# Layer 0's attention: the copy of a group's outputs one unit of squares later, and their turn one unit later

## The chip, the cores and the metric

One core of a Trainium2 chip runs the whole program. The metric is the time of one execution on the device in microseconds (us). The engines are named as in the profile: PE is TensorE (PEld its weight loads), ACT is ScalarE, DVE is VectorE, POOL is GpSimd, SP the queue that issues DMAs.

## What is computed

The program is two layers of a small model. Only the attention of layer 0 is touched: 1024 tokens, 16 heads of 16 columns, fourth-degree polynomial scores with a causal mask.

```python
a = jnp.einsum('bhnd,bhmd->bhnm', q, k) ** 4
a = jnp.tril(a)
denom = jnp.sum(a, axis=-1, keepdims=True)
out = jnp.einsum('bhnm,bhmd->bhnd', a / denom, v)
out = out.transpose(0, 2, 1, 3).reshape(b, n, e) @ w_out
```

After it come the mix into x, a layer norm, layer 1's attention and its mixture of experts. They wait for the attention's output.

## The kernel before

**Units.** The heads are worked in four groups g of four heads. A group has eight rows R = 8g + j, one for each block of 128 keys; row j needs queries from block j on. A row is cut into units: two heads by half of the row's width for j below 4, two heads by the whole width for j 4 and 5, four heads for j 6 and 7. There are 22 units in a group and 88 in all. A unit n passes through these steps:

- TensorE computes its scores into one of three pairs of PSUM banks (`scores0`, L609).
- ScalarE squares them out of PSUM into SBUF (L1109; semaphore `s0_sq`).
- VectorE squares the squares in place (L1437). For three units of a group ScalarE does it instead (L1112), always after it has done the next unit's first square.
- GpSimd masks the diagonal block of a unit that has one (L1818).
- TensorE multiplies a finished row by V (`out0`, L629) in two halves of the queries. It accumulates the group's outputs in banks 6 and 7.

**The end of a group.** ScalarE copies the group's outputs from banks 6 and 7 to `o_raw` (`copy_out0`, L1083). The first output product of the next group overwrites those banks, so `out0` waits for the copy (`o0_copied`). TensorE then turns `o_raw` in `turn_out0`: it takes a bank pair, runs `keep_clock(2, b)` (two matmuls nobody reads, four rows at L573), waits for the copy and does eight transposes (L641). VectorE divides by the denominators (`read_out0`, L1418 and L1420; `o0_ready`). When two groups are done, `turn_o(0)` turns their finished columns (L652), ScalarE's `high_o` and VectorE's `low_o` split the result in two parts (L1089, L1427; `oT_ready`). `add_nothing` (L578) adds products of zero to keep TensorE busy.

**The order.** `order0` writes TensorE's order out by hand: after the scores of unit n comes at most one output product. The output products of a row come LAG = 4 units after its last unit. `turned[n + 3]` places the turn. `PAIRED0` lists all steps that take a bank pair (scores, turn, turn_o) in TensorE's order, and the pairs rotate by three, so each step waits until the third before it has been read: scores by the square, a turn by `o0_ready`, a turn_o by `oT_ready`. ScalarE and VectorE run through the units in number order, with the special steps put in by dictionaries that are worked out from the same list: `COPY_AT` (ScalarE copies just before the square of that unit), `READ_AT` (VectorE divides just after that unit) and `SPLIT_O_AT` (both engines split just after that unit).

In the text s48 stands for the scores of unit 48 and q48 for their square on ScalarE; 4th47 is the fourth power of unit 47 on ScalarE, out16.0 the first half of row 16's output product, T1 the turn of group 1. Units 44 to 65 belong to group 2; unit 48, before whose square the copy of group 1 stands, is the first of group 2's second row, because the products run four units late.

Of the kernel before, what the change touches and what calls it, by code (L numbers as in the profile page):

```python
# [18 lines left out]
NT = TOK // P  # L19
# [7 lines left out]
H0, D0 = 16, 16  # L27
STK = 4 * D0
QUAD = 4
# [6 lines left out]
def units0(j):  # L36

    w = (NT - j) * P
    size = 2 if j < 6 else 4
    cuts = [(0, w // 2), (w // 2, w)] if j < 4 else [(0, w)]  # L40
    return [(list(range(i, i + size)), a, e) for i in range(0, QUAD, size) for a, e in cuts]


UNITS0 = [(R, *unit) for R in range(ROWS0) for unit in units0(R % NT)]
# [7 lines left out]
def order0():  # L52

    out, pieces, used, turned = [], [], None, {}
    for n in range(len(UNITS0) + LAG + 4):
        if n < len(UNITS0):
            out.append(("scores", n))
        for R in range(ROWS0):
            if DONE0[R] + LAG == n + 1:
                pieces += [("out", R, half) for half in range(NHALF) if R % NT < 4 * half + 4]  # L60
        for piece in pieces[:1 if n < len(UNITS0) else len(pieces)]:
            out.append(pieces.pop(0))
            if piece[1] % NT == NT - 1:
                turned[n + 3] = piece[1] // NT
        if n in turned:
            out.append(("turn", turned[n]))
            if turned[n] == H0 // QUAD // NC - 1:
                used = n + 4
        if n == used:
            out.append(("turn_o", 0))  # L70
    return out + [("turn", H0 // QUAD - 1)] * (("turn", H0 // QUAD - 1) not in out) + [("turn_o", 1)]


ORDER0 = order0()
PAIRED0 = [s for s in ORDER0 if s[0] != "out"]
PAIR_OF = {s: n % 3 for n, s in enumerate(PAIRED0)}


def last_scores(step):

    return max((s[1] for s in ORDER0[:ORDER0.index(step)] if s[0] == "scores"), default=0)


COPY_AT = {min(last_scores(("out", NT * g + NT - 1, 1)) + 1, len(UNITS0)): g for g in range(H0 // QUAD)}
READ_AT = {last_scores(("turn", g)): g for g in range(H0 // QUAD - 1)}
SPLIT_O_AT = last_scores(("turn_o", 0)) + 1
OUT_BANKS = [6, 7] + [2 * (3 - PAIR_OF["turn", H0 // QUAD - 1] - PAIR_OF["turn_o", 1]) + i for i in range(2)]
# [67 lines left out]
def build_program(nc, x_in, wqkv_in, wout_in, lns_in, lnb_in, packed_in, scales_in,  # L155
# [5 lines left out]
    with ExitStack() as ctx:  # L161
# [811 lines left out]
        def _(act):  # L973
# [105 lines left out]
            def copy_out0(g):  # L1079
                act.wait_ge(o0_used, NT * (g + 1))  # L1080
                if g >= 1:
                    act.wait_ge(o0_turned, g)
                act.activation(o_raw[:], psf[:, 3072:4096], ACT.Copy)\  # L1083
                    .then_inc(o0_copied, 1)
# [9 lines left out]
            for n in range(len(UNITS0)):  # L1094
                R, heads, a, e = UNITS0[n]
                w = e - a
                if n in COPY_AT:
                    copy_out0(COPY_AT[n])
                act.wait_ge(s0_ps, n + 1)
# [982 lines left out]
```

## Time and profile before

| what | value |
|---|---|
| time, median of 3 runs | 838.12 us (834.84, 838.12, 838.96) |
| time of the profiled execution | 838.65 us |
| its span, first to last instruction | 836.9 us |
| layer 0's attention stage in the span, about | 196.8 to 300.6 us |
| copies of the outputs (L1083) start at | 223.4, 248.4, 273.0, 295.2 us |

The time of an execution stands 1.75 us above its span; that part lies around the program. The three runs shown differ by 4.1 us, or 0.5%.

### The profile page before, as it was taken

What the parts mean: (1) busy time and instruction counts of PE and PEld (TensorE: products, weight loads), DVE (VectorE), ACT (ScalarE), POOL (GpSimd) and SP (SyncE); (2) the same over time, 40 slices, a digit from 0 to 9 for tenths busy, and PEclk for the clock granted to TensorE, in tenths of its full rate; (3) what the DMA queues carried; (4) which work ended last, traced back from release to release, by engine and by line L of the source; (5) the groups of instructions that cost most, each with busy time, mean ns of one, the idle gap of its engine ahead of it and who ended that gap; (6) DMA issues with size and microseconds to landing.
All of it is one profiled execution on the core that took longest, in us unless ns stands there. A gap on an engine that the chain in (4) does not pass through costs nothing.

```text
span 836.9 us, 14053 instructions
## 1 busy us (share of the span) xinstructions
PE 790.9 (95%) x4927; PEld 645.2 (77%) x4927; DVE 607.8 (73%) x1077; ACT 466.2 (56%) x822; POOL 424.0 (51%) x479
## 2 busy tenths in 40 slices
PE   6999999998889889998999999999999999999997
PEld 5777777765433367797999889989999999988885
DVE  8588869648989968778888688887767654445556
ACT  4433242359888833687656456655666655655431
POOL 1757846613554446455345433758565512655540
PEclk9999999999999999999999999999999999999999
DMA  5211186000000040000000000102010587743207
GB/s 186 69 45 38 39 255 182 1 1 1 1 1 2 1 129 26 26 7 26 7 20 7 8 20 7 58 26 65 21 51 26 200 200 266 279 149 104 57 2 251
DMA packets 50116, 59.82 MB, mean 71 GB/s; under 512 B 13559, under 2 KB 41084, under 8 KB 50048
## 3 DMA queue, kind: packets, MB, share of 16 engines
q1 hardware_dynamic: 45488, 50.49, 19.7%
q0 software_dynamic: 4560, 8.44, 2.8%
q8 instruction: 41, 0.67, 0.3%
q14 instruction: 27, 0.22, 0.1%
HBM read 41.11 MB, written 21.86 MB: 75 GB/s over the span
## 4 chain that ended last, share of the span: by engine, by line
PE 54%; DVE 11%; POOL 6%; ACT 6%; issue 4%; DMA 3%; SPq 0%; POOLq 0%; ACTq 0%; DVEq 0%
PE ps L802 12%; PE ps L517 8%; PE ps L519 8%; PE ps L518 8%; PE ps L895 4%; PE ps L926 3%; PE ps L892 3%; POOL A L1818 2%; DVE cap L1511 2%; DVE swap L1500 2%; PE ps L713 2%; PE ps L874 1%; DMA xa<-xg_scratch 1%; PE ps L559 1%; ACT A L1109 1%
## 5 line engine op out<-in xcount | busy, mean ns | idle before, releaser
L802 PE MATMUL ps<-V,P 128*128 128x129 f32 x1152 | 151.0, 277 | 0.0
L1161 ACT ACTIVATE cap<-cap 128x1024 f32<-128x1024 f32 (+7 forms) x128 | 87.3, 682 | 112.4 <-DVE cap L1511 106.9
L802 PEld LDWEIGHTS ps<-V,P 128*128 128x128 f32 x1152 | 143.6, 192 | 2.7
L1511 DVE SCALAR_TENSOR_TENSOR cap<-dist,ps 128x1024 f32<-128x1024 f32 (+7 forms) x128 | 95.4, 750 | 26.3 <-PE ps L519 22.9
L1742 POOL TENSOR_SCALAR_AFFINE_SELECT P<-P 128x128 f32<-128x128 f32 x128 | 39.4, 308 | 143.2 <-ACT P L1166 142.7
L1874 POOL DMA_INDIRECT y_scratch<-y_sb,aux_s x63 | 62.1, 985 | 61.8 <-issue 33.1
L1166 ACT ACTIVATE P<-cap 128x1024 f32<-128x1024 f32 (+7 forms) x128 | 87.9, 687 | 4.1
L517 PE MATMUL ps<-q_hi,k_hi 128*128 128x512 f32 x192 | 72.1, 376 | 6.8 <-DVE cap L1511 6.2
L519 PE MATMUL ps<-q_lo,k_hi 128*128 128x512 f32 x192 | 67.3, 351 | 0.0
L518 PE MATMUL ps<-q_hi,k_lo 128*128 128x512 f32 x192 | 66.9, 349 | 0.0
L517 PE MATMUL ps<-xT_hi,w_hi 128*128 128x512 f32 x128 | 56.4, 441 | 2.9 <-POOL w_lo L1762 1.9
L1667 DVE TENSOR_SCALAR gu<-ps 128x256 f32<-128x256 f32 (+1 forms) x63 | 28.9, 459 | 38.4 <-PE ps L895 15.9
L1849 POOL TENSOR_TENSOR rot<-rot,swap 128x512 f32<-128x512 f32 x40 | 52.1, 1302 | 8.7 <-DVE swap L1500 8.6
L1050 ACT ACTIVATE e_g<-ps 128x512 f32<-128x512 f32 x32 | 19.2, 599 | 66.2 <-PE ps L519 66.2
L1500 DVE TENSOR_TENSOR swap<-ps,sin 64x512 f32<-64x512 f32 x80 | 55.1, 688 | 1.1
L1437 DVE TENSOR_TENSOR A<-A 128x1024 f32<-128x1024 f32 (+2 forms) x40 | 49.6, 1287 | 4.5 <-ACT A L1109 4.5
L519 PE MATMUL ps<-xT_lo,w_hi 128*128 128x512 f32 x128 | 50.6, 395 | 0.0
L518 PE MATMUL ps<-xT_hi,w_lo 128*128 128x512 f32 x128 | 50.5, 394 | 0.0
L1198 ACT ACTIVATE sg<-gu 128x128 f32<-128x128 f32 (+1 forms) x63 | 20.5, 325 | 50.9 <-DVE gu L1667 46.3
L1109 ACT ACTIVATE A<-ps 128x1024 f32<-128x1024 f32 (+2 forms) x48 | 43.6, 967 | 9.1 <-PE ps L609 9.1
L517 PEld LDWEIGHTS ps<-q_hi,k_hi 128*128 128x128 f32 x192 | 36.5, 190 | 12.9 <-DVE cap L1511 4.8
L1857 POOL TENSOR_TENSOR q_lo<-rot,q_hi 128x512 fp32r<-128x512 f32 x32 | 41.4, 1293 | 9.0 <-ACT q_hi L1155 8.9
(293 smaller groups left out, 2100.6 us busy)
## 6 DMA issues: line engine op xcount, KB each, us to landing
xg_scratch<-blank SPq DMA_DIRECT2D x1, 8127.0 KB, 31.2
xa<-xg_scratch SPq DMA_DIRECT2D x63, 128.0 KB
ew<-in_experts SPq DMA_DIRECT2D x3, 1920.0 KB, 8.9
y<-y_scratch SPq DMA_DIRECT2D x8, 512.0 KB
pk<-in_packed SPq DMA_DIRECT2D x8, 384.0 KB, 3.1
pks<-in_scales SPq DMA_DIRECT2D x8, 384.0 KB, 4.0
ew<-in_experts SPq DMA_DIRECT2D x1, 3072.0 KB
wqk<-in_wqk SPq DMA_DIRECT2D x20, 128.0 KB
```

The source lines that it names most:

```text
L517: pe.matmul(o, l_hi, r_hi, start=start, stop=False)
L518: pe.matmul(o, l_lo, r_hi, start=False, stop=False)
L519: return pe.matmul(o, l_hi, r_lo, start=False, stop=stop)
L802: last = pe.matmul(ps[:, 4 + r % 2, o:o + D1 + 1], P1[:, h % 2, a:a + P], V1[:, j, h // REP, :], start=(j == 0), stop=(j == t))
L1109: act.activation(dst, src, ACT.Square).then_inc(s0_sq, 1)
L1161: act.activation(cap[:, CAP_AT[j]:CAP_AT[j] + w], cap[:, CAP_AT[j]:CAP_AT[j] + w], ACT.Tanh, scale=1.0 / (CAP * float(D1) ** 0.5))\
L1166: act.activation(P1[:, h % 2, OFF[j]:OFF[j] + w], cap[:, CAP_AT[j]:CAP_AT[j] + w], ACT.Exp, scale=CAP)\
L1437: dve.tensor_tensor(a, a, a, ALU.mult).then_inc(s0_four, 1)
L1500: last = dve.tensor_tensor(swap[to, i % 2, :], b[frm, :], sin1[frm, tk], ALU.mult)
L1511: dve.scalar_tensor_tensor(out=cap[:, CAP_AT[j]:CAP_AT[j] + w], in0=dist[:, 0:w], scalar=slope, in1=psf[:, 1024 * (n % 2):1024 * (n % 2) + ...
L1849: pool.tensor_tensor(r, r, swap[:, i % 2, :], ALU.add).then_inc(pj_rot, 1)
L1874: pool.indirect_dma_start(out=y_dram, out_offset=bass.IndirectOffsetOnAxis(ap=aux_s[:, b, 0:1].bitcast(U32), axis=0), in_=y_sb[:, b % YRIN ...
```

## The change

The turn of groups 0 to 2 goes one unit later in TensorE's order. The first output product of the next group has a fixed place, so it now stands ahead of the turn. ScalarE's copy goes one unit later: one more square is done ahead of it. The last group's copy and turn stand where they stood, because its place is cut off at the number of units. What follows from the order moves too:

| | before | after |
|---|---|---|
| copy ahead of the square of unit | 26, 48, 70, 88 | 27, 49, 71, 88 |
| TensorE around T1 | s48 s49 s50 T1 s51 out16.0 s52 out16.1 s53 | s48 s49 s50 s51 out16.0 T1 s52 out16.1 s53 |
| VectorE divides after unit | 28, 50, 72 | 29, 51, 73 |
| turn_o(0) in TensorE's order | s54 turn_o s55 out17.0 s56 | s54 s55 out17.0 turn_o s56 |
| both engines split after unit | 55 | 56 |

Units 29, 51 and 73 are fourth-powered by ScalarE, so VectorE has no work of its own between the two places, and its division stands where it stood.

```diff
             if piece[1] % NT == NT - 1:
-                turned[n + 3] = piece[1] // NT
+                turned[n + 4] = piece[1] // NT
...
-COPY_AT = {min(last_scores(("out", NT * g + NT - 1, 1)) + 1, len(UNITS0)): g for g in range(H0 // QUAD)}
+COPY_AT = {min(last_scores(("out", NT * g + NT - 1, 1)) + 2, len(UNITS0)): g for g in range(H0 // QUAD)}
```

## Rows read from the trace of the kernel before

**Rows 1.** The page: busy us (share of the span) and instructions of each engine.
```profile
PE 790.9 (95%) x4927; PEld 645.2 (77%) x4927; DVE 607.8 (73%) x1077; ACT 466.2 (56%) x822; POOL 424.0 (51%) x479
```

**Rows 2.** Busy time of each engine from copy 1 to copy 2.
```profile
core 0: us, PE busy (x) PEld busy (x) DVE busy (x) ACT busy (x) POOL busy (x), PEclk, DMA share, GB/s
248.40:273.00 24.60, 21.84 (x172) 9.37 (x170) 22.51 (x24) 21.84 (x30) 12.15 (x15) 1.00 0.00 1
```

**Rows 3.** The chain that ended last, over the stage: start, us, what.
```profile
261.06 2.30 DVE stack L1437 x3
...
264.76 4.83 POOL A L1818 x4
...
272.98 0.26 ACT o_raw L1083
```

**Rows 4.** Timeline of ACT around copy 1: start, us, instruction [idle before <-releaser].
```profile
248.37 1.02 ACT L1083 ACTIVATE o_raw<-ps 128x1024 f32<-128x1024 f32 x1
249.28 0.92 ACT L1109 ACTIVATE A<-ps 128x896 f32<-128x896 f32 x1
250.07 1.07 ACT L1112 ACTIVATE A<-A 128x1024 f32<-128x1024 f32 x1
251.02 2.59 ACT L1109 ACTIVATE A<-ps 128x896 f32<-128x896 f32 x3
254.06 0.81 ACT L1109 ACTIVATE qk_tok<-ps 128x768 f32<-128x768 f32 x1 [0.45 <-PE ps L609]
...
255.61 2.38 ACT L1109 ACTIVATE qk_tok<-ps 128x768 f32<-128x768 f32 x3
```

**Rows 5.** Timeline of PE around T1.
```profile
248.09 0.92 PE L609 MATMUL ps<-QT,KT 64*128 64x448 f32 x6
250.25 1.13 PE L573 MATMUL ps<-x_tok 128*128 128x256 f32 x4 [1.25 <-ACT A L1109]
251.22 1.04 PE L641 MATMUL ps<-ident,o_raw 128*128 128x128 f32 x8
252.18 0.47 PE L609 MATMUL ps<-QT,KT 64*128 64x448 f32 x2
252.58 1.06 PE L629 MATMUL ps<-A,V 128*32 128x512 f32 x8
253.58 0.44 PE L609 MATMUL ps<-QT,KT 64*128 64x384 f32 x2
```

**Rows 6.** Timeline of PE, ACT and DVE around turn_o(0) and its split.
```profile
257.07 0.85 PE L629 MATMUL ps<-A,V 128*32 128x384 f32 x8
257.89 1.08 ACT L1089 ACTIVATE xT_hi<-ps 128x512 fp32r<-128x512 f32 x2
258.51 1.29 DVE L1427 TENSOR_TENSOR xT_lo<-ps,xT_hi 128x512 fp32r<-128x512 f32 x2 [0.23 <-ACT xT_hi L1089]
258.84 0.73 ACT L1109 ACTIVATE stack<-ps 128x640 f32<-128x640 f32 x1
...
259.43 0.87 ACT L1112 ACTIVATE qk_tok<-qk_tok 128x768 f32<-128x768 f32 x1
...
259.86 0.71 PE L609 MATMUL ps<-QT,KT 64*128 64x320 f32 x6 [0.60 <-DVE xT_lo L1427]
260.32 1.90 ACT L1109 ACTIVATE stack<-ps 128x640 f32<-128x640 f32 x3
```

**Rows 7.** Timeline around T0, the same steps a group earlier.
```profile
225.29 1.75 PE L573 MATMUL ps<-x_tok 128*128 128x256 f32 x4 [1.25 <-ACT A L1109]
226.84 1.92 PE L641 MATMUL ps<-ident,o_raw 128*128 128x128 f32 x8
...
230.73 0.81 ACT L1109 ACTIVATE qk_tok<-ps 128x768 f32<-128x768 f32 x1 [0.44 <-PE ps L609]
```

**Rows 8.** A window around T0; the columns of rows 2.
```profile
226.00:229.00 3.00, 3.00 (x13) 2.35 (x11) 2.44 (x3) 1.80 (x3) 0.41 (x1) 0.50 0.00 0
```

**Rows 9.** Timeline of ACT behind T2.
```profile
278.68 0.81 ACT L1109 ACTIVATE qk_tok<-ps 128x768 f32<-128x768 f32 x1 [0.45 <-PE ps L609]
```

## The prediction

> **What bounds the kernel now.** I read the page first: PE is busy for 95% of an 836.9 us span [rows 1], but that is a mean over stages. So I asked for the stage that the change touches, from one copy of a group's outputs to the next. In those 24.6 us PE is busy for 21.84 us, DVE for 22.51 us and ACT for 21.84 us [rows 2]. No engine is the bound alone, so the chain of work that ended last has to say what the order costs. It leads from the copy through ACT and PE to VectorE's fourth powers at 261.06, from there on through DVE and four masks on POOL (4.83 us), and so to the next copy at 272.98 [rows 3]. Two things follow. What delays the fourth powers at 261.06, or their like in another group, delays the group by as much, since DVE runs on without idle time behind them. And what ACT loses ahead of them is not made up, since the squares feed DVE one by one. Behind the stage all work waits for its last output, so a microsecond lost here is one lost in the end.
>
> Then the timelines of ACT and PE around copy 1 [rows 4, 5]. ACT has no idle time from 248.37 to the end of its three squares at 251.02 + 2.59 = 253.61; it stands for 0.45 us before q52. PE stands for 1.25 us before T1, because T1's bank pair is the one that q48 reads, and q48 comes behind the copy. I call the distance from one start to the next on an engine the step of an instruction: it is shorter than the record, since these overlap.
>
> **The change around copy 1, step by step.** Nothing is added or removed; it is the same instructions in another order.
>
> - *ACT.* q48 needs s48, which PE starts at 248.09; two such matmuls take 0.47 us and an activation starts 0.04 us behind them (253.58 + 0.44 to 254.06) [rows 4, 5]. So q48 starts at 248.60 where the copy started at 248.37. 4th47 follows after q48's step of 0.79, at 249.39, the copy after another 0.95, at 250.34. It ends at 251.36; it ended at 249.39. The three squares q49 to q51 start 0.91 later, at 251.25, and end at 253.84, which is 0.23 later than before.
> - *PE.* s51 takes a pair that q48 frees at 249.52, so it is done inside the wait, by 250.04. This step of 0.40 (252.18 to 252.58) is what the new order gains. But the next instruction in the queue is out16.0, and it needs banks 6 and 7, which are free only when the copy ends: 251.36 and 0.05 for the release (250.20 to 250.25 before) gives 251.41 [rows 4, 5]. All that is queued behind waits with it. Then out16.0 takes its step of 1.00, keep_clock 0.97 and the transposes 0.96 [rows 5]. T1's own wait is for q49, over at about 252.2, so it costs nothing. s52 starts at 251.41 + 2.93 = 254.34, where it started at 253.58: later by 0.76. The short form: PE's work starts 1.16 us later and has 0.40 us less to do.
> - *Who waits.* q52 goes to 254.82; ACT's idle time before it grows from 0.45 to 1.0 us. VectorE's division follows T1 with nothing moved past it, and what waits for it is s54, two units of scores further on. No DMA is issued by any moved step, and no queue of SP or POOL is passed.
>
> So a group whose turn is moved loses **0.76 us** up to its fourth powers. In group 2 the picture of before is the same, down to the 0.45 us of idle time [rows 9], so T2 costs 0.75 us as well.
>
> **Around T0** the clock comes in. PE's granted clock is 0.50 from 226 to 229, and 1.00 over all of the next group [rows 2, 8]: TensorE ran at 1.2 GHz there and at 2.4 GHz here. keep_clock's and the transposes' records are 1.75 and 1.92 us long there, against 1.13 and 1.04 around T1 [rows 5, 7]. From the copy to the unit behind the turn it is 230.73 - 223.41 = 7.32 us, and 254.06 - 248.37 = 5.69 us around T1 [rows 4, 7]: such a fall costs 1.63 us. What PE did before it fell is the same as around T1: a wait of 1.25 us and then keep_clock. If the clock falls at the same instant in the changed kernel, out8.0 starts at 223.41 + 3.04 = 226.45 and has a step of 2.0 at 1.2 GHz, keep_clock starts at 228.45. The low clock lasts to about 229.1 (the transposes' end is at 228.76, and the window at 229 still shows it), so 0.64 us of keep_clock run at it, which is 0.32 of its work of 0.97, and 0.65 are left at the full one, then 0.96 for the transposes and 0.44 for s30: 231.14. q30 starts at 231.18, against 230.73: **0.45 us** lost where a fall is there before and after, and 0.75 where there is none in either.
>
> **The turn of the finished columns** moves too, and this is the dearest part. After T1's delay, q52 stands at 254.82 and q53 1.55 behind it, at 256.37 (254.06 to 255.61); 4th51, which runs between them, ends as q53 starts, by 256.5 [rows 4]. turn_o now comes behind out17.0. That product needs 4th51, and its record is 0.85 long, so turn_o starts at 257.3; it is eight transposes as T1 is (a step of 0.96), so s56 starts at 258.3 and q56 about 0.45 behind it, at 258.8, where it was [rows 6]: up to here the delay is made up, because the split no longer stands ahead of q56. But 4th55 now comes ahead of the split as well. It starts 0.59 behind q56 (258.84 to 259.43), at 259.4, and ScalarE's split 0.77 later (0.87 of record less 0.1), at 260.14, where it started at 257.89. VectorE's part ends 1.91 behind that (257.89 to 259.80), at 262.05. Its end frees the bank pair: before for s57 at 259.86, after for s58. So s58 starts at 262.11, and q58 at 262.56 (0.46 behind, as 260.32 behind 259.86), where q58 stood 0.6 behind 260.32, at 260.91. ACT stands idle for 0.8 us in front of it. The fourth power of unit 58 stood second of the three that take 2.30 us, at about 261.06 + 0.74 = 261.80. It now follows q58's end, 262.56 + 0.70, at 263.3: 1.5 us later, and DVE goes on from there [rows 3, 6]. The 0.76 of T1 are contained in this, so group 1 loses **1.5 us**.
>
> **Sum.** 0.45 + 1.5 + 0.75 = 2.7 us. The last group and its end are unchanged. Against the profiled execution this is 838.65 + 2.7 = 841.35 us. That execution stands 0.53 us above the median, so on the median it is 838.12 + 2.7 = **840.8 us**, or 0.3% slower. What measurement can tell from no change here is about 0.5%, or 4.2 us. The two unknown sizes are bounded so: a plain turn costs between 0 (PE's work fits into the wait) and 1.16 (nothing of it is gained), the split between 0.76 (only T1's delay goes on) and 2.25 (its whole shift from 257.89 to 260.14 goes on). That is 0.8 to 4.6 us for the three; I take the values read off step by step, as every step of them has a row of its own shape beside it.
>
> **Rivals.**
>
> - *The clock falls more often* (slower; the other side of no difference). Between s50's end at 249.0 and out16.0 at 251.41 PE now has 1.9 us without work, with only s51 inside, where it had 1.25 us. The row shows that 1.25 us was enough around T0 and not around T1 and T2, so the place is close to the edge already. Each further fall costs 1.63 us less the 0.3 that T0's delay shrank by, so 1.3 to 1.6: 842.3 with one, 843.7 with two. It decides from the first further fall on, since 2.7 + 1.5 reaches 4.2 us. For it speaks the longer idle time in all three places; against it that keep_clock still stands right behind. The Trainium skill ("TensorE: Matmul & The Clock Gate", A second HAM failure mode: psum-queue depth-cycling) says that short idles of PE between groups of matmuls, as it cycles through PSUM banks, are enough to make the clock oscillate. By that rule, the trace agrees at one place in three. Chance 0.25.
> - *The clock no longer falls.* The matmuls of s51 now stand inside the wait and may keep it up around T0. Then 838.12 + 0.75 + 1.5 + 0.75 - 1.63 = 839.5 us. Against it speaks that the idle time in all is longer. Chance 0.10.
> - *Something else sets the group's length.* If POOL's four masks (4.83 us) with DVE beside them had slack ahead of them, the delay would end there and nothing would change: 838.1 us. The chain speaks against it: it passes from DVE to POOL without an idle piece [rows 3]. Chance 0.10.
> - *Faster.* The old copy stood ahead of q48 and made PE wait 1.25 us. If TensorE's early scores were worth more than I count, at best all 0.45 us of ACT's idle time at three places and the one fall would go, 3.0 us: 835.1 us. It would need out16.0 not to wait for the copy. Chance 0.05.
> - *The forecast*, with as many falls as before: 0.50.
>
> **Range and chances.** From 838.0, the case that nothing changes, to 843.5, nearly two further falls, it holds all but the faster case and the far ends. Slower by over 0.5% is above 842.3: most of the first rival and the upper end of the forecast's bounds, 0.25. Faster by over 0.5% is below 833.9, which no case reaches, 0.04 for what I have not seen. Within 0.5% is 0.71.
>
> **What would show it.** In the profile after, the first instruction of PE behind the copy must be L629, waiting for the copy, 3.0 us after the end of q47; the square behind the turn must stand 6.45 us after the old place of the copy (5.69 before). In group 1 the six score matmuls at 259.86 no longer wait for xT_lo; the next ones do, and ACT idles 0.8 us there. The distance between the copies must grow by 0.75 and 1.5. A granted clock of 0.50 around T1 or T2 would speak for the first rival. The prediction is wrong if the distance between copies stays at 24.6 us though PE waits longer.

## The result and the profile after

The changed kernel takes 843.1 us in the median of 11 runs (839.83 to 846.94), the kernel before 837.41 us in 11 (833.97 to 841.85). The ratio is 1.0072, with a 95% interval of 1.0052 to 1.0093: slower by 6.0 us, between 4.4 and 7.8. The forecast was 2.7 us slower. The time lies in the stated range, near its upper end (843.5). It is beyond what the prediction counted as no difference (842.3), a case to which it had given a chance of 0.25, against 0.71 for no difference.

The profiled execution after took 846.91 us, one of the slowest of the 11. The page:

```profile
span 845.2 us, 14053 instructions
PE 793.5 (94%) x4927; PEld 646.3 (76%) x4927; DVE 604.9 (72%) x1077; ACT 465.8 (55%) x822; POOL 425.5 (50%) x479
```

As many instructions as before and nearly the same busy time in each engine; the span is longer by waits [rows 1]. Around T1, PE's timeline after; these are the lines that answer to [rows 5]:

```profile
247.29 0.90 PE L609 MATMUL ps<-QT,KT 64*128 64x448 f32 x6
248.78 0.47 PE L609 MATMUL ps<-QT,KT 64*128 64x448 f32 x2 [0.59 <-ACT A L1109]
250.64 1.07 PE L629 MATMUL ps<-A,V 128*32 128x512 f32 x8 [1.38 <-ACT o_raw L1083]
251.63 1.13 PE L573 MATMUL ps<-x_tok 128*128 128x256 f32 x4
252.60 1.04 PE L641 MATMUL ps<-ident,o_raw 128*128 128x128 f32 x8
253.57 0.45 PE L609 MATMUL ps<-QT,KT 64*128 64x384 f32 x2
```

s51 runs inside the wait, out16.0 waits 1.38 us for the copy, and then everything follows with the steps of before. ACT's timeline at the same place answers to [rows 4]:

```profile
248.62 1.05 ACT L1112 ACTIVATE A<-A 128x1024 f32<-128x1024 f32 x1
249.57 1.01 ACT L1083 ACTIVATE o_raw<-ps 128x1024 f32<-128x1024 f32 x1
250.47 2.53 ACT L1109 ACTIVATE A<-ps 128x896 f32<-128x896 f32 x3
254.05 0.81 ACT L1109 ACTIVATE qk_tok<-ps 128x768 f32<-128x768 f32 x1 [1.05 <-PE ps L609]
```

From 4th47 to q52 it is 254.05 - 248.62 = 5.43 us; the prediction had 254.82 - 249.39 = 5.43. ACT's idle time before q52 is 1.05 us, as forecast (1.0; it was 0.45).

At the split of the turned columns, PE, ACT and DVE after; the answer to [rows 6]:

```profile
259.40 1.08 ACT L1089 ACTIVATE xT_hi<-ps 128x512 fp32r<-128x512 f32 x2
260.02 1.29 DVE L1427 TENSOR_TENSOR xT_lo<-ps,xT_hi 128x512 fp32r<-128x512 f32 x2 [0.40 <-ACT xT_hi L1089]
...
261.37 0.30 PEld L609 LDWEIGHTS ps<-QT,KT 64*128 64x128 f32 x4 [2.23 <-DVE xT_lo L1427]
261.37 0.56 PE L609 MATMUL ps<-QT,KT 64*128 64x320 f32 x4 [2.00 <-DVE xT_lo L1427]
261.83 1.30 ACT L1109 ACTIVATE stack<-ps 128x640 f32<-128x640 f32 x2 [0.75 <-PE ps L609]
...
263.15 1.93 PE L629 MATMUL ps<-qk_tok,V 128*32 128x512 f32 x8
```

The wait for xT_lo stands in front of s58 as forecast and costs ACT 0.75 us of idle time (forecast 0.8). But look at PE: it stands for 2.00 us there, and two instructions on, the product at 263.15 has a record of 1.93 us, where its like takes 1.06 [rows 5]. That is the clock, which the windows show (columns of [rows 2]):

```profile
225.50:228.00 2.50, 2.50 (x11) 0.96 (x4) 2.09 (x2) 1.87 (x3) 0.05 (x1) 0.50 0.00 0
250.50:254.50 4.00, 3.86 (x30) 2.11 (x30) 2.88 (x4) 2.95 (x5) 0.75 (x2) 1.00 0.01 2
262.60:265.60 3.00, 3.00 (x12) 0.81 (x14) 2.75 (x3) 1.55 (x2) 0.93 (x1) 0.50 0.00 0
279.60:282.60 3.00, 3.00 (x12) 2.30 (x10) 1.43 (x2) 0.92 (x2) 0.41 (x1) 0.50 0.00 0
```

PE ran at 1.2 GHz at T0, at the split of group 1 and at T2, and at 2.4 GHz at T1. Before it ran at 1.2 GHz at T0 alone [rows 2, 8]. I call a stretch with a granted clock of 0.50 a low window, and what begins it a fall of the clock.

I measure the stage from the start of the first score matmul to the start of the last copy. Before, that is 98.4 us (from 196.8 to 295.2, the last time in the table above). After:

```profile
L609 PEld LDWEIGHTS ps<-QT,KT x192: 182/183/334, 195.3 to 293.5; 64*128 64x128 f32 x192
L1083 ACT ACTIVATE o_raw<-ps x4: 1015/1016/1024, 223.9 to 299.7; 128x1024 f32<-128x1024 f32 x4
```

With two decimals of the timelines it is 299.68 - 195.34 = 104.3 us, against 98.38 before: 6.0 more. All stages below are taken with two decimals. The two traces differ by 8.3 us in their spans. The rest lies outside the stage: it begins 1.5 us earlier after, and behind it 3.8 us more were spent. The changed lines do not reach those parts. In the nine traces of this document the part behind the stage takes 537.7 to 545.5 us, and it is not long where the stage is long (539.0 behind the longest stage, of 110.4). So I don't explain that rest by the change.

### The profile page after: what moved, and what is told of

Its sections match the earlier page's. It is cut to its first block, busy times and chain, and to the rows that moved or that the text cites. A ratio compares the mean times of both kernels' runs of the same rounds, so it can differ in the third digit from the quotient of the medians.

```text
span 845.2 us, 14053 instructions
## 1 busy us (share of the span) xinstructions
PE 793.5 (94%) x4927; PEld 646.3 (76%) x4927; DVE 604.9 (72%) x1077; ACT 465.8 (55%) x822; POOL 425.5 (50%) x479
## 4 chain that ended last, share of the span: by engine, by line
PE 56%; DVE 11%; ACT 6%; POOL 6%; issue 5%; DMA 1%; SPq 0%; POOLq 0%; ACTq 0%; DVEq 0%
PE ps L802 12%; PE ps L517 8%; PE ps L519 8%; PE ps L518 8%; PE ps L895 4%; PE ps L892 3%; PE ps L926 2%; DVE cap L1511 2%; DVE swap L1500 2%; PE ps L629 2%; POOL A L1818 2%; PE ps L713 2%; PE ps L559 1%; PE ps L874 1%; POOL rot L1849 1%
## 5 line engine op out<-in xcount | busy, mean ns | idle before, releaser
L1511 DVE SCALAR_TENSOR_TENSOR cap<-dist,ps 128x1024 f32<-128x1024 f32 (+7 forms) x128 | 95.3, 750 | 25.6 <-PE ps L519 22.1
```

What stands on the lines that cost most here:

```text
L1511: dve.scalar_tensor_tensor(out=cap[:, CAP_AT[j]:CAP_AT[j] + w], in0=dist[:, 0:w], scalar=slope, in1=psf[:, 1024 * (n % 2):1024 * (n % 2) + ...
```

## The experiments

The theory that stood at the outset: the order costs 3.0 us where no fall of the clock is counted (0.75 + 1.5 + 0.75), and the rest of the 6 us is TensorE's clock, which falls more often because PE has longer idle time. The rival is that the longer waits, or the copy's or the turn's place, cost more by themselves than the steps say. A stage without a fall takes 98.4 - 1.63 = 96.75 us in the kernel before by this theory. The experiments were timed in two sets, each beside 29 runs of the kernel before: the first four with a median of 835.88 us for that kernel, the last three with 836.94 us. Each ratio is to the kernel before of its own set.

### The copy alone later

```diff
-                turned[n + 4] = piece[1] // NT
+                turned[n + 3] = piece[1] // NT
```

(Against the changed kernel.)

> The copy one unit later alone; TensorE's order stays as in the kernel before. Reading by order: T1 gets its pair from q48 at 249.5 and runs keep_clock while the copy runs, so its transposes start when the copy ends (251.4) and all behind it is 0.2 us later per group, 0.6 us in the stage. From the stage's first scores to the last copy 97.3 us without a fall of the clock (96.75 before, worked out as 98.38 less one fall of 1.63), plus 1.6 per fall. Ratio 1.000 to 1.002. The rival that the copy's place itself is what costs: ratio near 1.004 or more.

Measured: ratio 0.9991, interval 0.9975 to 1.0008. The stage in its trace, and PE at T1:

```profile
L609 PEld LDWEIGHTS ps<-QT,KT x192: 182/183/187, 195.7 to 287.0; 64*128 64x128 f32 x192
L1083 ACT ACTIVATE o_raw<-ps x4: 1016/1017/1024, 224.3 to 293.2; 128x1024 f32<-128x1024 f32 x4
```
```profile
248.95 1.09 PE L641 MATMUL ps<-ident,o_raw 128*128 128x128 f32 x8 [0.73 <-ACT o_raw L1083]
249.97 0.47 PE L609 MATMUL ps<-QT,KT 64*128 64x448 f32 x2
```

The stage takes 97.5 us, with a granted clock of 1.00 in all its windows. The forecast was 97.3. PE waits in two parts with keep_clock between them. So the copy's place costs 0.7 us of order and no clock in this trace, and nothing that the timing can tell. The rival that blames the copy falls.

### The turn alone later

```diff
-COPY_AT = {min(last_scores(("out", NT * g + NT - 1, 1)) + 2, len(UNITS0)): g for g in range(H0 // QUAD)}
+COPY_AT = {min(last_scores(("out", NT * g + NT - 1, 1)) + 1, len(UNITS0)): g for g in range(H0 // QUAD)}
```

> The turn one unit later alone, with turn_o(0) and its split moved as in the changed kernel; ScalarE's copy stays in its old place. Reading by order: out16.0 finds the copy done, s51 and out16.0 run before T1 instead of behind it, and s52 starts where it did: T0 and T2 cost nothing. The split still comes behind q56 and 4th55 and costs 0.7 us in group 1. Stage 97.5 us without falls, 1.6 more per fall; PE keeps its 1.25 us wait at each turn and gets a wait of about 2 us at the split, where a fall is likely. Ratio 1.001 to 1.003. Rival (the turn's place costs by itself): 0.75 per group, stage 99 us and over.

Measured: 1.0076, interval 1.0048 to 1.0103 (6 runs). That is the whole loss again, against my expectation of 1.001 to 1.003. PE at T1:

```profile
250.38 0.91 PE L609 MATMUL ps<-QT,KT 64*128 64x448 f32 x6
252.54 0.47 PE L609 MATMUL ps<-QT,KT 64*128 64x448 f32 x2 [1.25 <-ACT A L1109]
253.68 1.93 PE L629 MATMUL ps<-A,V 128*32 128x512 f32 x8 [0.68 <-ACT A L1112]
255.54 2.08 PE L573 MATMUL ps<-x_tok 128*128 128x256 f32 x4
257.41 1.91 PE L641 MATMUL ps<-ident,o_raw 128*128 128x128 f32 x8
259.26 0.69 PE L609 MATMUL ps<-QT,KT 64*128 64x384 f32 x2
```

The copy starts at 250.66 in this trace and is over at 251.68, so out16.0 does not wait for it. It waits for its other input, 4th47 (L1112), and starts 253.68 - 250.66 = 3.02 us behind the copy's start: just when it would in the changed kernel (251.41 - 248.37 = 3.04 in the prediction's times). ScalarE does the copy, q48 and 4th47 in either kernel before out16.0 can start, and only their order differs. I had overlooked that wait. Then out16.0, keep_clock, the transposes and s52 all run at 1.2 GHz. Four windows, one at each of the three turns and one at the split:

```profile
224.00:230.00 6.00, 4.26 (x19) 1.71 (x16) 4.77 (x5) 5.03 (x6) 1.61 (x4) 0.65 0.00 0
251.00:257.00 6.00, 4.07 (x18) 1.60 (x16) 4.58 (x4) 4.85 (x6) 1.44 (x4) 0.68 0.00 1
265.00:271.00 6.00, 4.00 (x24) 1.26 (x24) 4.14 (x6) 4.32 (x7) 1.34 (x2) 0.65 0.00 0
282.00:288.00 6.00, 4.30 (x17) 1.56 (x16) 4.62 (x5) 5.26 (x7) 1.33 (x4) 0.66 0.01 3
```

The mean clock is about 0.66 in all four. The stage takes 110.4 us (197.24 to 307.65). This trace is of the slowest of the six runs, 848.34 us; their median is 843.34.

### turn_o(0) and its split back at their old places

```diff
-                used = n + 4
+                used = n + 3
```

> The changed kernel with turn_o(0) and the split at their old places (behind s54 and unit 55). Reading by order: group 1 loses 0.76 instead of 1.5 us, so the stage is 99.0 us without falls; against the changed kernel's trace the distance from copy 1 to copy 2 falls from 27.5 to about 25.4 us, since the 2 us wait of PE at the split and the fall in it go too. Ratio 1.003 to 1.006 with two falls left. If the split costs nothing by itself, the distance stays within 0.3 us of 27.5.

Measured: 1.0033, interval 1.0013 to 1.0054. From copy 1 to copy 2 it is 26.6 us; after it was 27.5. A fall stands inside the distance (the window at T1):

```profile
251.50:254.50 3.00, 2.49 (x10) 0.74 (x11) 1.79 (x3) 2.88 (x4) 0.72 (x2) 0.51 0.00 0
```

The fall of the changed kernel stood at the split and this one stands at T1, so this pair of traces has a fall on both sides, and 0.9 us is what the split costs beside it. That bears out the sign; the size needs a kernel without falls (below). My 25.4 us had none in it; with a fall of 1.6 us it would be 27.0, so the trace is 0.4 us shorter. The whole stage is 104.8 us in this trace, no shorter than in the changed kernel, because the clock was low for longer at T0: from T0's copy to T1's it is 27.0 us, against 25.6 in the changed kernel. So no gain shows in this one trace; the timed runs show one, though the two intervals touch (1.0013 to 1.0054 here, 1.0052 to 1.0093 for the changed kernel).

### The waits filled

The changed kernel, with two matmuls nobody reads ahead of s29, s51, s73 and s57. They write to the bank pair that those scores overwrite.

```diff
-                bank_pair(("scores", n))
+                keep_clock(2 * (n in (29, 51, 57, 73)), bank_pair(("scores", n)))
```

> The changed kernel with two matmuls nobody reads ahead of s29, s51, s73 (inside the wait for the copy) and ahead of s57 (inside the wait for the split): about 1 us of idle time of TensorE is filled at each of the four places, nothing else waits for them. If the excess over the 3.0 us of the order is clock (three falls in the trace after, one before): no window of granted clock 0.50 in the stage, stage 99.8 us instead of 104.3, ratio 1.001 to 1.003. If the longer waits cost the excess without the clock: the stage stays near 104 us, ratio 1.007.

Measured: 1.0028, interval 1.001 to 1.0046. Windows over the stage, and its ends:

```profile
196.00:224.00 28.00, 24.41 (x173) 9.49 (x172) 24.91 (x24) 24.73 (x33) 13.89 (x15) 1.00 0.00 1
224.00:250.00 26.00, 23.37 (x172) 10.12 (x172) 23.37 (x23) 22.60 (x29) 13.79 (x15) 1.00 0.00 1
250.00:277.00 27.00, 24.07 (x184) 10.83 (x186) 22.74 (x24) 22.82 (x30) 13.68 (x16) 1.00 0.01 2
277.00:299.00 22.00, 20.62 (x162) 9.44 (x155) 16.15 (x18) 14.66 (x20) 9.03 (x11) 1.00 0.08 16
```
```profile
L609 PEld LDWEIGHTS ps<-QT,KT x192: 182/183/187, 196.7 to 290.5; 64*128 64x128 f32 x192
L1083 ACT ACTIVATE o_raw<-ps x4: 1016/1017/1024, 225.3 to 296.6; 128x1024 f32<-128x1024 f32 x4
```

The clock is 1.00 throughout and the stage takes 99.9 us; 99.8 was expected. The matmuls that nobody reads take 4.4 us out of the stage. What PE waits for comes no earlier for it:

```profile
250.47 1.07 PE L629 MATMUL ps<-A,V 128*32 128x512 f32 x8 [0.33 <-ACT o_raw L1083]
261.19 0.56 PE L609 MATMUL ps<-QT,KT 64*128 64x320 f32 x4 [0.94 <-DVE xT_lo L1427]
```

The copy starts at 249.40 here, so out16.0 starts 1.07 us behind it, as in the changed kernel (250.64 - 249.57), and s58 starts 11.8 us behind it, as there (261.37 - 249.57). The order's delays are still there and only their idle time is partly filled, so it was the clock and not the waits that made the difference. Over the runs, the mean granted clock of this kernel is 0.9962, that of the kernel before beside it 0.9960: with the clock no lower it is still 2.3 us slower (0.8 to 3.8). That is the order's part, 3.2 us in the traces.

### The turn alone, filled

As the turn alone, with such pairs of matmuls, fillers from here on, ahead of s28, s50, s72 and s57.

> The turn alone one unit later (as in the run with the copy in its old place), with two matmuls nobody reads ahead of s28, s50, s72 and s57, so that the clock stays up. Its unfilled form showed out16.0 starting 3.03 us behind the copy's start, held by the fourth power of unit 47 on ScalarE, not by the copy: as late as in the changed kernel (3.04). If that is the cost of the order, the stage takes about 99.9 us here (96.75 + 0.75 + 1.5 + 0.75 and a little for the fillers), as with the changed kernel filled, ratio 1.002 to 1.004, and all the rest of the 110.4 us of the unfilled form was clock. If the turn's place costs nothing by itself (my first reading), the stage takes 97.5 us, ratio 1.000 to 1.001.

Measured: 1.0026, interval 1.0006 to 1.0045; stage 100.1 us, against 110.4 unfilled. So 10.3 us of that stage were clock, and the turn's place costs as much order as turn and copy together. Over the runs the gain is smaller: the kernel is 0.76% slower than the one before without the fillers and 0.26% with them, which is some 4 us. PE at T1:

```profile
249.10 1.07 PE L629 MATMUL ps<-A,V 128*32 128x512 f32 x8 [0.71 <-DVE A L1437]
```

The copy starts at 246.04 here; out16.0 starts 3.06 us behind it. The profile puts the wait down to VectorE's fourth power of unit 48, which ends then. The code does not wait for that unit. 4th47 ends 0.3 us earlier, at 248.81, and is the only input of out16.0 that ends late; the unfilled trace names it. I take it to be the cause by the code, and did not test it by itself.

### turn_o(0) back, filled

> The changed kernel with turn_o(0) and its split at their old places and fillers ahead of s29, s51, s73. If the place of the split costs 0.75 us by itself, the stage takes 99.1 to 99.2 us without falls (99.93 with the split moved) and the distance from copy 1 to copy 2 is 25.4 to 25.5 us (26.26 with it moved). If the split costs nothing once the clock is kept, the stage stays at 99.9. Ratio 1.001 to 1.003.

Measured: ratio 1.0016, interval 0.9996 to 1.0037. The stage:

```profile
L609 PEld LDWEIGHTS ps<-QT,KT x192: 182/183/187, 196.7 to 289.5; 64*128 64x128 f32 x192
L1083 ACT ACTIVATE o_raw<-ps x4: 1015/1016/1024, 225.4 to 295.7; 128x1024 f32<-128x1024 f32 x4
```

That is 98.9 us. From copy 1 to copy 2 it is 25.2 us, against 26.3 us with the split moved and filled. The split's place costs 1.0 us by itself, forecast as 0.75. This kernel has no filler ahead of s57, but that one delays nothing in the other (s58 starts at the same distance from the copy with it and without it, above).

### The kernel before, filled

```diff
-                bank_pair(("scores", n))
+                keep_clock(2 * (n in (28, 50, 72)), bank_pair(("scores", n)))
```

> The kernel before with two matmuls nobody reads ahead of s28, s50 and s72, inside the wait of 1.25 us. If one fall costs 1.63 us and nothing else changes, the stage takes 96.8 us instead of 98.38, and the median is up to 1 us below the one before, which has such a fall in some of its runs only: ratio 0.9985 to 1.000. If the fillers delay the turn, the stage is longer than 96.9 us without a fall and the ratio is 1.000 or above.

Measured: 0.999, interval 0.997 to 1.0009. The stage:

```profile
L609 PEld LDWEIGHTS ps<-QT,KT x192: 182/183/187, 195.4 to 286.0; 64*128 64x128 f32 x192
L1083 ACT ACTIVATE o_raw<-ps x4: 1019/1022/1024, 222.0 to 292.1; 128x1024 f32<-128x1024 f32 x4
```

That is 96.7 us, as the 96.75 worked out for the kernel before without its fall. It bears out the price of the fall at T0: 98.38 - 96.74 = 1.64 us. Over the runs, the mean granted clock of the whole program is 0.9978 with the fillers and 0.9958 without them, a share worth 1.7 us. The median is 0.95 us lower, and the interval holds no difference at all, so no kernel here beats the one before measurably.

All stages side by side, in us, each from one trace; the last column is the mean granted clock of the whole program, over all runs of the kernel that have it on record:

| kernel | stage | granted clock of 0.50 in it | mean clock of the runs |
|---|---|---|---|
| before | 98.4 | T0 | 0.9960 and 0.9958 (29 each) |
| before, filled | 96.7 | nowhere | 0.9978 (12) |
| copy alone | 97.5 | nowhere | 0.9969 (12) |
| turn_o back, filled | 98.9 | nowhere | 0.9977 (12) |
| changed, filled | 99.9 | nowhere | 0.9962 (12) |
| turn alone, filled | 100.1 | nowhere | 0.9976 (12) |
| changed | 104.3 | T0, split, T2 | 0.9924 (11) |
| turn_o back | 104.8 | T0 (long), T1, T2 | 0.9944 (12) |
| turn alone | 110.4 | all four, long | 0.9887 (6) |

## Why the prediction was right, and where it fell short

**The order's cost, by its steps.** It was right around T1, T2 and the split, step by step. The trace after has the distance from 4th47 to q52 at 5.43 us as worked out, the new wait for the copy in front of out16.0, ACT's idle time at 1.05 us (forecast 1.0) and 0.75 us at the split (0.8). The sum can be read without the clock: changed and filled, less before and filled, is 99.9 - 96.7 = 3.2 us. The prediction's terms without a fall make 0.75 + 1.5 + 0.75 = 3.0. Of the terms, the split was a little dearer than forecast: 1.0 us and not 0.75 beyond T1's delay.

The 0.45 us for T0 was too low. It rested on the clock falling at the same instant as before and coming back at the same instant. ACT after, around T0:

```profile
222.98 1.05 ACT L1112 ACTIVATE A<-A 128x1024 f32<-128x1024 f32 x1
...
229.94 0.81 ACT L1109 ACTIVATE qk_tok<-ps 128x768 f32<-128x768 f32 x1 [2.57 <-PE ps L609]
```

From 4th25 to q30 it is 229.94 - 222.98 = 6.96 us, where the prediction had 231.18 - 224.43 = 6.75 (its 4th25 stands 1.02 behind the old place of the copy). So T0 lost 0.66 us, and a fall in the changed kernel gives back less of the delay than the 0.3 us that the prediction took off.

**The reason for the new wait was right, but did not carry over.** In the changed kernel out16.0 waits for the copy, as predicted: 4th47 has ended 0.9 us earlier (248.62 + 1.05 = 249.67, against 249.57 + 1.01 = 250.58 for the copy). With the copy back ahead of q48 the two change places, 4th47 ends last, and out16.0 starts as late as in the changed kernel. So the conclusion that I drew for the second experiment, that with the copy in its old place the turn would cost nothing, was wrong.

**The term that was mis-sized is the clock.** The forecast put as many falls after as before, and gave 0.25 to the rival "the clock falls more often". That rival is what happened. In the trace the stage has three low windows instead of one. 104.3 - 99.9 = 4.4 us go to three falls, 1.5 us each in the mean, in the range of 1.3 to 1.6 that the rival named, and 98.38 - 96.74 = 1.64 us went to one before (1.63 forecast). From copy 1 to copy 2, where the fall at the split lies, it is 27.5 us against 26.3 filled, so that one cost 1.3 us. Over all runs: the mean granted clock of the 11 runs is 0.9924, and that of the 58 runs of the kernel before beside the experiments 0.9959. Those runs were not made side by side with the 11. A share of 0.0035 of 843 us is 3.0 us, and with the 3.0 us of the order this makes the 6.0 us of the ratio. So the forecast's mechanism explains half of the loss. That the time lies in the range comes from its upper end, which was drawn for the rival, and in part from luck: the 11 runs of the kernel before have a median of 837.41 us, 0.7 below the 838.12 that the forecast added to, and 6.0 us on top of 838.12 would have been 844.1, outside the range.

**Which step let it through.** The prediction compared PE's idle time at the turn (1.9 us against 1.25) and found the place "close to the edge already", but weighed this against the keep_clock that still followed. It also looked only at ACT's 0.8 us at the split; it never asked how long PE stands there. PE stands 2.00 us in front of s58, until 261.37, and the second low window begins 1.0 us later. With the split back at its old place the ratio was 1.0033 and the mean clock 0.9944, against 1.0072 and 0.9924. The argument against the rival did not hold. With keep_clock behind the wait the clock fell all the same: at T0 its mean was already 0.56 between 224.8 and 225.0 us, before the wait was over, and keep_clock began at 226.9. With pairs of fillers inside the waits there is no low window in the stage, in four kernels with one trace each.

**The rivals that fell.** The clock did not stay up because s51 stands in the wait: it fell at T0 and T2 with s51's like inside. Nothing else sets the group's length, since the delays on ACT came out in the stage (3.2 us against 3.0). Nor was the kernel faster.

The rule of the Trainium skill ("TensorE: Matmul & The Clock Gate", A second HAM failure mode: psum-queue depth-cycling) that short idles of PE between groups of matmuls can make the clock oscillate agrees with three of the four places in the trace after: the longest idle record of PE in front of a low window was 1.39 us at T0 and T2, and 2.00 us at the split. At T1 it was 1.38 us and the clock stayed up, and no run here shows what told T1 from T0 and T2.

## What to carry to other kernels

When steps are reordered on an engine that has to wait, write down the idle time of TensorE at every place, not only of the engine that sets the pace. A wait that costs 0.75 us by its order cost another 1.5 us by the clock where the clock fell. Filling the wait before its end, with work into a bank that is about to be overwritten, showed in one run which part was order and which was clock. And before saying that an instruction waits for one thing, list all its inputs with the time at which each is due.

## What the runs showed of the hardware

The granted clock fell and stayed up at places with nearly the same wait in the same trace. Before, it fell after 1.25 us of waiting at T0 and not after 1.25 us at T1 and T2. After, it fell around waits of 1.39 us at T0 and T2 and not after 1.38 us at T1. With the turn alone later, where PE waits 1.25 us and then 0.4 to 0.7 us with one pair of score matmuls between, it was low at all three turns and at the split. The stage grew by 10.3 us over the same kernel with the waits partly filled, in the slowest of six runs. I had expected such a kernel to lose a fall or two. What decides at which of such places the clock falls stays open.
